# An attention and feed-forward layer on one core: the projection products of a step between the two halves of its scores, its context products last

## The reference

```python
def block(x, inner):
    return x + layernorm(inner(layernorm(x)))

def attention(h):                      # h: (8, 512, 512)
    q, k, v = (heads(h @ W + b) for W, b in ((Wq, bq), (Wk, bk), (Wv, bv)))
    probs = softmax(q @ k.T / 4)       # 32 heads, 512 x 512 each
    return join(probs @ v) @ Wo + bo

def ffn(h):                            # weights rounded to fp8 values
    return ((silu(h @ gate_w * gate_scale) * (h @ up_w * up_scale)) @ down_w) * down_scale
```

## Time and profile before

| | |
|---|---|
| median of 3 runs | 1712.83 us (1712.39 to 1716.59) |
| the profiled execution: its own time | 1714.72 us |
| its span in the trace | 1712.9 us |
| mean granted TensorE clock | 0.977 of full speed |
| busy share of the span: PE, DVE, ACT, POOL | 93%, 70%, 53%, 36% |
| the chain that ended last: PE, DVE, ACT | 61%, 24%, 8% |

### The profile page before, as it was taken

How to read it: one execution, slowest core, us unless ns; L and a number is a source line. 1 busy time by engine, 2 the same in 40 slices (tenths; PEclk the granted TensorE clock), 3 DMA queues, 4 the chain that set the end, 5 groups by cost and what they waited for, 6 DMA issues and landing times.

```text
span 1712.9 us, 22893 instructions
## 1 busy us (share of the span) xinstructions
PE 1585.2 (93%) x8266; PEld 728.8 (43%) x8266; DVE 1191.8 (70%) x2200; ACT 908.0 (53%) x1624; POOL 619.7 (36%) x504
## 2 busy tenths in 40 slices
PE   4899999999999999999999999879999999999996
PEld 3433333333334334333333433215555555555553
DVE  6698898898888888888888888764254353353433
ACT  3177676666766767767767766672222222222221
POOL 4124343533633542542443352143332232232331
PEclk9799999999999999999999999979999999999998
DMA  3412212312211312321221121510201201201110
GB/s 115 102 37 72 52 45 71 88 50 65 79 56 50 97 35 60 91 55 51 84 73 49 46 81 41 164 56 19 87 25 50 74 25 49 75 25 50 50 50 25
DMA packets 81740, 105.63 MB, mean 62 GB/s; under 512 B 16214, under 2 KB 46934, under 8 KB 81624
## 3 DMA queue, kind: packets, MB, share of 16 engines
q1 hardware_dynamic: 81628, 104.17, 20.8%
HBM read 52.71 MB, written 21.50 MB: 43 GB/s over the span
## 4 chain that ended last, share of the span: by engine, by line
PE 61%; DVE 24%; ACT 8%; issue 5%; DMA 1%; POOL 1%; SPq 1%; POOLq 0%; ACTq 0%; DVEq 0%
PE ring L1371 19%; PE side L1001 13%; DVE maxima L832 11%; PE down_sums L1385 10%; PE contexts L1076 8%; PE scores L1063 6%; PE maxima_scores L1040 4%; ACT probs L741 3%; DVE channel_shift_bits L971 2%; DVE channel_shift_bits L969 1%; DVE denominators L857 1%; DVE qkT L816 1%; DVE stats_in L787 1%; DVE y L823 1%; DVE ctx_raw L862 1%
## 5 line engine op out<-in xcount | busy, mean ns | idle before, releaser
L832 DVE TENSOR_REDUCE maxima<-maxima_scores 128x1 f32<-128x512 f32 x1024 | 655.5, 679 | 92.7 <-PE maxima_scores L1040 87.4
L741 ACT ACTIVATE probs<-scores 128x512 f32<-128x512 f32 x1024 | 549.4, 601 | 283.8 <-PE scores L1063 283.1
L1040 PE MATMUL maxima_scores<-k_stack,q_stack 64*128 64x512 f16 x1024 | 340.2, 390 | 47.2 <-DVE maxima L832 46.7
L1063 PE MATMUL scores<-q_stack,k_stack 64*128 64x512 f16 x1024 | 326.8, 390 | 14.2 <-ACT probs L741 8.1
L1076 PE MATMUL contexts<-probs,v_around_ones 128*32 128x512 f32 x2048 | 278.7, 616 | 8.4 <-ACT denominators L685 3.5
L1321 DVE SCALAR_TENSOR_TENSOR fuse<-ring,up_scale,gate 128x512 f32<-128x512 f32 x96 | 72.0, 750 | 292.9 <-PE ring L1371 284.2
L1235 POOL TENSOR_TENSOR fuse_low<-fuse,fuse_high 128x512 fp32r<-128x512 f32 x96 | 137.8, 1436 | 372.7 <-ACT fuse_high L1257 372.7
L1257 ACT CAST fuse_high<-fuse 128x512 fp32r<-128x512 f32 x96 | 59.4, 619 | 291.9 <-PE down_sums L1385 270.0
L1063 PEld LDWEIGHTS scores<-q_stack,k_stack 64*128 64x128 f16 x1024 | 65.5, 94 | 339.6 <-ACT probs L741 183.2
L1385 PE MATMUL down_sums<-down_q,fuse_high 128*128 128x512 f32 x384 | 168.0, 437 | 1.1 <-issue 0.8
L1371 PE MATMUL ring<-xT_high_ffn,gate_q 128*128 128x512 f16 x384 | 146.6, 382 | 7.4 <-DVE xT_low_ffn L1294 5.9
(11 more groups left out here) (201 smaller groups left out, 2409.4 us busy)
## 6 DMA issues: line engine op xcount, KB each, us to landing
q_stack<-qkT SPq DMA_DIRECT2D x192, 64.0 KB, 2.0
k_stack<-qkT SPq DMA_DIRECT2D x192, 64.0 KB, 2.0
x_rows<-in_L_attn_hidden_states SPq DMA_DIRECT2D x8, 1024.0 KB, 5.3
x_residual<-in_L_attn_hidden_states SPq DMA_DIRECT2D x32, 256.0 KB, 2.9
middle_rows<-y SPq DMA_DIRECT2D x32, 256.0 KB, 3.3
x_rows_ffn<-middle_rows SPq DMA_DIRECT2D x8, 1024.0 KB, 5.6
x_residual_ffn<-middle_rows SPq DMA_DIRECT2D x8, 1024.0 KB, 7.9
out_rows<-y_ffn SPq DMA_DIRECT2D x32, 256.0 KB, 2.2
```

The lines of the kernel that those rows point to most:

```text
L741: act.activation(probs[:, n % 2, j, :], work[(b * (GH * STEPS) + GH * n + j) % RING][:], ACT.Exp, scale=float(D) ** -0.5).then_inc(p_full, 1)
L832: dve.tensor_reduce(maxima[:, g % 2, at:at + 1], bank[:], AX.X, ALU.max).then_inc(rot_free, 1)
L1040: mm = pe.matmul(bank[:], q_st[half, s, qc * P:qc * P + P], k_st[half, s, :], start=True, stop=True)
L1063: mm = pe.matmul(work[i % RING][:], k_st[half, s, c * P:c * P + P], q_st[half, s, :], start=True, stop=True)
```

## The change

The order of TensorE's instructions in a step is changed, and nothing else. The projection pieces move from the end of the step to between the second and the third pair of score and maxima product. The contexts of the step before move from there to behind the fourth pair. The same instructions are issued, with the same waits; the lists of the other engines are unchanged.

```diff
@@ -1128,10 +1128,11 @@
                         score(b, n, j)
                         if beside:
                             rot_item(items[j][1], items[j][0])
-                    if u == 0 and n:
-                        contexts(b, n - 1)
-                for c in range(lo, hi):
-                    side_piece(side_at[(what, i), later], later, (what, i), c)
+                    if u == 0:
+                        for c in range(lo, hi):
+                            side_piece(side_at[(what, i), later], later, (what, i), c)
+                if n:
+                    contexts(b, n - 1)
                 for item, of in items[beside:]:
                     rot_item(of, item)
             contexts(b, STEPS - 1)
```

## The result

The changed kernel takes **1994.6 us** (median of 3 runs, 1990.9 to 1995.4), against 1712.8 before: 1.163 times as long, 95% interval 1.160 to 1.167. The forecast was 1938 with a range of 1840 to 2050. The direction is as forecast and the time lies in the range; the loss is larger than the point forecast: 282 us of loss by the medians where 223 were forecast. All of the difference is in the attention turns: the feed-forward products begin 276 us later than before, and the spans differ by 276.

The account below looks back on a forecast made before the run. TensorE and VectorE were both taken as close to full (129.0 and 118.5 of a 136.9 us turn). Six middle turns' 189 us, the first's 20 and the last's 14 made 223 on 1714.7: 1938 us, range 1840 to 2050.

Parts of the forecast that it names:

- The wait at a new item: In odd steps, TensorE stands 1.27 us before the projection pieces until the take ends; 16 in a turn.
- The late reads: Reads of later contexts delay takes: VectorE's in steps 8, 16, 24 cost 7.2 us a turn, ScalarE's 3.1.
- The clock: TensorE's clock falls at long waits: 8 falls of 1.5 us are 12 a turn, cut to 8 us.
- a fall in every pair: Rival: TensorE's clock falls in each pair of steps, 24 us a turn instead of 8; 2058 us, chance 0.12.
- The sum of a middle turn: A full turn: 160.4 us at full clock plus 8 for the clock, 168.4 against 136.9, so +31.5.
- 32 bare steps: A turn's steps without any wait, 3.66 us each: 117.1 us.
- the clean waits: TensorE's waits of 1.27 us at new items with nothing further delaying the take, 16 in a turn.
- the later terms: Further delays of takes in a turn: late reads 7.2 and 3.1, turn's end 1.6, other VectorE work 6.5 and 4.6.
- The outer turns: First turn +20 us, with 10 takes waited for; last turn +14 in all, with eight takes and some delayed reads.
- Six middle turns: The second to the seventh turn, together 189 us of the forecast loss.
- later terms are hidden: Rival: only clean stalls, three reads and the turn's end cost; a turn of 146.2 us, 1790 us in all, chance 0.06.
- Faster: Rival: pieces fill TensorE's waits, 2.4 us of it at the turn's end; about 10 a turn, 1635 us, chance 0.03.

Follow-up runs that it names:

- x12: The changed kernel with only VectorE's two reads of the odd contexts moved later, behind the fourth reduction and the next step's first: 1910.7 us.
- x4: The changed kernel with the take moved to behind the third reduction of the step in which the item ends, ScalarE's high part also earlier: 1732.2 us.
- x5: The changed kernel with six extra copies of the third score product ahead of each new item's first piece: 1944.7 us.
- x1: The kernel before, with TensorE's step order made four pairs, projection pieces, contexts: 1946.8 us.
- x2: The kernel before, with TensorE's step order made two pairs, contexts, pieces, two pairs: 1908.1 us.
- x13: The kernel before, with TensorE's step order made four pairs, contexts, pieces: 1823.7 us.
- x8: The kernel before, with only VectorE's take moved from behind the first reduction of a step to behind the third: 1835.2 us.

## Why the prediction was right, and where it was off

- **The wait at a new item.** Right in place and count, and in size where it is clean: 16 in a turn; 1.26 us against 1.27 forecast; an odd step of 4.99 us against 4.93; over the whole span 229 us in 114 waits, where 116 were named (the first turn has 10, as the sum had it, and not 12). Only five of the 16 are near the clean size, the others are 2.1 to 3.5 us. That it is the cause, and not only beside the cause, is shown by the early take, which keeps TensorE's order and loses 36.4 of the 37.7 us.
- **The late reads.** Right as a mechanism. VectorE waited 2.1 us at most and 5.8 a turn, in the three steps named and at the turn's end. Their direct price was 4.8 us a turn by the later reads alone, against 7.2 for this item in the sum; through TensorE's busy time, at the lower clock, they cost another 7.2. In the sum I kept the two apart, and x12 shows that they aren't independent.
- **The clock: the term that was too small.** I put 8 falls at 1.5 us and wrote off 4 of the 12, for what lies beside VectorE's backlog and for the fall that the turn before has. The price of a fall was right (1.53 us in step 23). Both deductions were wrong: in step 23 nothing of it was hidden, and the turn before holds its own fall inside its 136.9 us, so to take it off a sum at full clock counts it twice. By the estimate above it is 9 falls and 13.8 us where 8 stood. The clock in the turns was 0.91 where "about 0.93" was written. The rival (a fall in every pair, 24) did not come: around the clean wait of the timeline above (638.3 to 641.7, and the 3.4 us before) the granted clock was 1.00. In the middle turns the falls followed waits of 1.5 to 3.5 us, and not each of them (step 23). x4 and x5 show that the clock comes back with the waits gone or filled. The Trainium skill ("TensorE: Matmul & The Clock Gate", section "A second HAM failure mode: psum-queue depth-cycling") says that frequent small idle times between groups of products can make the clock swing. This trace bears it out only in part: here the clock swings, but the idle times of 1.26 us left it alone.
- **The sum of a middle turn** was 168.4 us, and 174.2 were measured. Less the 13.8 us of the clock that is 160.4, the sum without its clock term, and in this luck had a part. The sum is 32 bare steps (117.1), the clean waits (20.3) and the later terms (23.0). Measured, the waits beyond the clean ones are 32.8 - 20.3 = 12.5 us, with 3.0 more before maxima products: 15.5 where 23.0 stood. The waits at steps 9, 17 and 25, behind the three reads, and at 15 were called 3 to 5 us and measured 2.1; the take behind step 12 was put 9.3 us after that step's first score and came at 8.3, since the two scalings there take 0.43 us each and not 0.81, which is a mean over short and long ones. About as much was missing on the other side: the turn before has nearly 20 us beyond 32 bare steps (its fall of the clock among them), of which the sum took over next to nothing, and some 7 us of it are still there, among them the transposes (0.58 us from 646.72 to 647.30). The two errors cancelled. This comparison rests on the estimated number of falls.
- **The outer turns.** Relative to their size the forecast was off most here. From first score to first score, the first turn took 155.1 us instead of 127.8, 27 more where 20 were forecast; the last, to its last context product, 154.2 instead of 129.9, 24 more where 14 were forecast. In the last the clock was 0.81 against 0.90 before (windows above); I had sized that turn by its takes and reads and given the clock nothing in it. No run separates the clock from the waits there.
- **Six middle turns** carry, counted in this way, 224 of the 276 us; the sum had 189.
- The rival "later terms are hidden" (146.2 us a turn) is excluded by the turn's length, though a third of those terms did not show. "Faster" named a real gain: the pieces in step 0 do give 2.4 us a turn, the figure worked out there, but only when they wait for nothing.

What my working did not contain is the alternation. The order before puts 1.0 us of contexts and 1.6 us of pieces alternately between two pairs, so outside step 0 the two rings of three banks are never asked for four products at once. The changed order keeps this alternation; x1, x2 and x13 break it and cost 14 us a turn and more, of which waits for takes explain only a part in x2, little in x1 and nothing in x13. That the missing alternation is the reason fits the waits for the rings in x13, but it was not isolated.

## What to carry to other kernels

When work is moved earlier on an in-order engine, look at the first wait that it brings forward and ask at which time the release comes, counted from the same start; if that release is queued on another engine behind products that now stand behind the wait, the loss is up to the full difference in each round (16.2 of 21.3 us in x8), and moving the release (here VectorE's take and the ScalarE copy that it needs) can give back nearly all that the move cost. Late results hurt twice when their reader stands ahead of such a release. When a turn is added up from bare steps, carry over also what the turn before had beyond them, and subtract nothing from it twice. And between two rings that other engines drain, it looks best to alternate the blocks that fill neither.

## What the runs showed of the hardware that I had not expected

More work made the kernel faster: 96 useless products a turn, put into TensorE's waits, shortened the turn by 7.1 us, because the granted clock rose from 0.91 to 0.96. And an edit that took away only 4.8 us of waiting (x12) returned 12.1, the rest through shorter products at the higher clock. The same step with the same wait of 2.1 us took 5.87 us in one turn and 7.40 in the next, where the clock fell; and whole turns with equal waits alternated between 172.5 and 175.7 us.
